# The softplus sum of a hybrid Mamba and RWKV block on TensorE instead of GpSimd and VectorE

## The reference

```
xs, z = split(x @ W_in.T)                         # 512 channels each
xc = silu(conv4(xs) + conv_b)
dt, Bm, Cm = split(xc @ W_x.T, [64, 80])
dt = softplus(dt @ W_dt.T + b_dt)                 # what the change touches
h[t] = exp(dt*A) * h[t-1] + dt * Bm * xc          # 16 states for each of 512 channels
y = (sum_n h*Cm + D*xc) * silu(z);  out = y @ W_out.T
ffn: (silu(x @ Wg.T) * (x @ Wu.T)) @ Wd.T         # 768 hidden
rwkv: e = exp(clip(W + K)); A/B by cumulative sums of e*V and e; (sigmoid(R) * A/B) @ Wo.T
```

## Time and profile before

| | us |
|---|---|
| timed runs (3) | median 1663.07, from 1662.47 to 1665.38 |
| profiled execution, its own time | 1667.68 |
| its span, first to last instruction | 1665.9 |
| TensorE busy in the span | 1518.8 (91%) |
| VectorE | 1467.1 (88%) |
| GpSimd | 1313.8 (79%) |
| ScalarE | 1211.1 (73%) |
| weight loads of TensorE | 748.9 (45%) |

### The profile page before, as it was taken

How to read it: one execution, slowest core, us unless ns; L and a number is a source line. 1 busy time by engine, 2 the same in 40 slices (tenths; PEclk the granted TensorE clock), 3 DMA queues, 4 the chain that set the end, 5 groups by cost and what they waited for, 6 DMA issues and landing times. The chain is left out here.

```text
span 1665.9 us, 19103 instructions
## 1 busy us (share of the span) xinstructions
PE 1518.8 (91%) x5026; PEld 748.9 (45%) x5026; DVE 1467.1 (88%) x1997; ACT 1211.1 (73%) x1993; POOL 1313.8 (79%) x693
## 2 busy tenths in 40 slices
...
GB/s 228 186 202 124 158 150 134 129 151 102 137 153 230 41 128 160 129 207 120 126 159 213 121 119 158 152 183 114 106 155 170 178 88 126 100 57 62 74 45 32
DMA packets 163519, 225.22 MB, mean 135 GB/s; under 512 B 13458, under 2 KB 104083, under 8 KB 163411
## 3 DMA queue, kind: packets, MB, share of 16 engines
...
...
## 5 line engine op out<-in xcount | busy, mean ns | idle before, releaser
L921 POOL TENSOR_TENSOR bu<-rep,bc 128x1024 f32<-128x1024 f32 x256 | 600.4, 2363 | 140.2 <-PE ps_y L1449 65.9
L1085 ACT ACTIVATE ps_d<-rep,scale_a 128x512 f32<-128x512 f32 x512 | 338.4, 684 | 155.1 <-DVE bu L1262 101.1
L1385 PE MATMUL ps_r<-xT,wgu 128*128 128x512 f32 x768 | 351.3, 603 | 7.8 <-ACT xT L1093 2.2
L1255 DVE TENSOR_TENSOR_SCAN ps_d<-ps_d,bu 128x512 f32<-128x512 f32 x272 | 322.6, 1214 | 11.9 <-ACT ps_d L1085 8.3
L927 POOL TENSOR_TENSOR bu<-bu,bc 128x1024 f32<-128x1024 f32 x120 | 282.9, 2363 | 20.1 <-DVE bu L1255 18.9
L1255 DVE TENSOR_TENSOR_SCAN bu<-ps_d,bu 128x512 f32<-128x512 f32 x240 | 285.3, 1209 | 15.0 <-POOL bu L921 10.3
L1385 PE MATMUL ps_r<-mix,wkv 128*128 128x512 f32 x512 | 247.9, 616 | 26.9 <-ACT kv L1122 12.6
L962 ACT ACT_TABLE_LOAD x191 | 245.1, 1283 | 3.4
L1385 PEld LDWEIGHTS ps_r<-xT,wgu 128*128 128x128 f32 x768 | 141.5, 191 | 210.2 <-issue 197.8
L940 POOL TENSOR_TENSOR kv<-sums,kv 128x1024 f32<-128x1024 f32 x64 | 150.7, 2354 | 46.3 <-DVE sums L1352 45.7
L1262 DVE TENSOR_TENSOR bu<-ps_d,bc 128x512 f32<-128x512 f32 x272 | 178.2, 678 | 1.0
...
## 6 DMA issues: line engine op xcount, KB each, us to landing
rep<-dd_scratch SPq DMA_DIRECT2D x128, 512.0 KB, 5.1
...
```

The lines of the kernel that those rows point to most:

```text
L921: pool.tensor_tensor(bu[:, i % BU:i % BU + 2, :], rep[:, g % REP:g % REP + 2, 1, :], bc[:, 0, q, :].unsqueeze(1).to_broadcast([P, 2, T]), ...
L1085: act.activation(ps_d[D_BANK[i]][:, :], rep[:, g % REP, 0, :], ACT.Exp, scale=scale_a[:, a, NQ * j + q:NQ * j + q + 1]).then_inc(decay_rea ...
L1255: dve.tensor_tensor_scan(states, d[:, :], bu[:, i % BU, :], 0.0, ALU.mult, ALU.add)\
L1385: last = pe.matmul(dst, lhs, rhs, start=n == 0, stop=n == len(pairs) - 1)
```

## The change

The three additions leave GpSimd and VectorE. A new unit `p_sum` on TensorE multiplies the four tensors relu(a), e, 1 - u and ln(u) by the identity and accumulates them in the bank that held the `p_dt` of the tile; a new unit `a_sp` on ScalarE copies the bank into the dd slot. GpSimd keeps the product with xc, now for sequence 0 too, and VectorE has no part in dt any more. `a_ln` of the next tile waits for p_sum instead of dt. The bank is released by dt_ready, raised by the copy, instead of sp_relu.

```diff
@@ released
-                "p_xproj": (xdbl_ready, 1), "p_dt": (sp_relu, i + 1),
+                "p_xproj": (xdbl_ready, 1), "p_dt": (dt_ready, i + 1),
@@ GpSimd, g_dt
-                        pool.wait_ge(sp_neg.sem, at(sp_neg, m, i + 1))
-                        pool.tensor_tensor(rest_u, dtx, rest_u, ALU.add).then_inc(sp_rest.sem, 1)
-                        pool.wait_ge(sp_rest.sem, at(sp_rest, m, i + 1))
-                        pool.tensor_tensor(lnu, lnu, rest_u, ALU.add).then_inc(sp_sum.sem, 1)
-                        pool.wait_ge(sp_sum.sem, at(sp_sum, m, i + 1))
-                        pool.tensor_tensor(dt, dt, lnu, ALU.add).then_inc(dt_ready.sem, 1)
                         pool.wait_ge(dt_ready.sem, at(dt_ready, m, i + 1))
                         pool.tensor_tensor(dtx, dt, xc[:, i, :], ALU.mult).then_inc(dtx_ready.sem, 1)
@@ ScalarE, a_ln
-                            act.wait_ge(dt_ready.sem, at(dt_ready, m, i))
+                            act.wait_ge(sp_sum.sem, at(sp_sum, m, i))
@@ ScalarE
+                    elif unit == "a_sp":
+                        act.wait_ge(sp_sum.sem, at(sp_sum, m, i + 1))
+                        act.copy(dd_slot(i)[:, 0, :], ps_r[BANK[m, "p_dt", i]][:, :]).then_inc(dt_ready.sem, 1)
@@ VectorE: the whole of v_dt (three additions and the product) is gone
@@ TensorE
+                    elif unit == "p_sum":
+                        bank = ps_r[BANK[m, "p_dt", i]]
+                        pe.wait_ge(sp_relu.sem, at(sp_relu, m, i + 1))
+                        pe.wait_ge(sp_neg.sem, at(sp_neg, m, i + 1))
+                        for n, part in enumerate((dd_slot(i)[:, 0, :], dd_slot(i)[:, 1, :], rest_u, lnu)):
+                            last = pe.matmul(bank[:, :], ident[:, :], part, start=n == 0, stop=n == 3)
+                        last.then_inc(sp_sum.sem, 1)
@@ ORDER and BANKS: written anew for all five lists; the first words of "p"
-        "hp_turn*2 p_in*7 p_xproj p_dt p_in p_dt*2 p_warm*4 p_dt p_warm*25 hp_turn p_y hp_turn p_in p_y p_in*3 "
+        "hp_turn*2 p_in*7 p_xproj p_dt p_in p_dt*2 p_sum p_dt p_warm*4 p_sum p_warm*6 p_sum p_warm*3 p_y p_sum "
```

More of the change, by code:

```diff
@@ L65 @@
 COUNTS = {
-    "a_dt": JD, "a_in": JD, "a_ln": JD, "a_xc": JD, "a_xproj": 1,  "ha_std": 2, "ha_norm": 2,
+    "a_dt": JD, "g_dt": JD, "p_sum": JD, "a_sp": JD, "a_in": JD, "a_ln": JD, "a_xc": JD, "a_xproj": 1,  "ha_std": 2, "ha_norm": 2,
     "ha_turn": KC, "hp_turn": KC, "hv_stats": 2, "hv_aggr": 2, "p_dt": JD, "p_in": 2 * JD, "p_xproj": 1, "s_dt": JD,
@@ new lines @@
+        "p_warm p_y p_in*3 p_y fp_turn p_warm*4 p_y fp_turn2 fp_turn fp_turn2 p_in*2 p_xproj p_in p_dt p_y p_k "
+        "p_v p_sum p_y p_recept*5 p_k p_dt p_recept p_k p_v p_y p_dt p_sum p_y p_v p_recept*2 p_k p_v p_dt "
+        "p_warm*3 p_k p_y p_sum p_v p_k p_y p_sum p_post p_k p_v p_y p_post p_wo p_wo2 p_wo p_wo2 fp_turn p_v p_y "
+        "fp_turn2 fp_turn fp_turn2 p_k fp_gate fp_up fp_gate fp_up p_y fp_gate p_y fp_up hp_turn fp_gate fp_up "
+        "fp_gate fp_up fp_gate fp_up hp_turn p_v p_in*2 p_y*2 fp_down fp_down2 fp_down fp_down2 p_in*2 p_y p_wo "
@@ new lines @@
+        "fp_gate fp_up p_k fp_gate p_y p_dt fp_up p_v fp_gate fp_up p_sum hp_turn*2 p_y fp_down fp_down2 fp_down "
+        "fp_down2 p_wo p_wo2 p_wo fp_turn fp_turn2 fp_turn fp_turn2 p_wo2 p_y p_in*2 p_y p_k p_in rp_turn "
+        "rp_turn2 p_in rp_turn rp_turn2 p_v p_in p_y p_in*2 p_xproj p_in p_k p_v p_dt p_y p_recept*2 p_sum p_y "
+        "p_recept p_k p_v p_y p_dt p_recept rp_gate p_sum rp_up rp_gate rp_up p_y p_k p_v p_recept rp_gate rp_up "
+        "p_recept rp_gate rp_up p_y rp_gate*2 rp_up p_k rp_up p_y p_v p_recept rp_down rp_down2 p_recept p_y "
```

501 lines of the change are left out of this document (246 added, 255 removed), and 118 rows, old and new, of tables (BANKS, ORDER).

## The result

| | before | after |
|---|---|---|
| median, us (9 runs each) | 1662.47 | 1670.26 |
| lowest to highest | 1658.86 to 1665.38 | 1667.00 to 1676.92 |
| ratio, 95% interval | | 1.0044 [1.0029, 1.0059] |
| profiled execution, its span | 1667.68, 1665.9 | 1671.08, 1669.3 |

The change costs 7.8 us, 0.44%: slower, as forecast, but by a quarter of the 29 us.

What follows compares the result with a forecast made beforehand. TensorE and VectorE were near-bounds in the middle, TensorE alone in the tail. The middle gave +29 us, other terms 0: 1697 on the profiled 1667.7, less 4.6 to the median, 1692 us; range 1660 to 1722.

Steps and rivals of the forecast that it cites:

- The full share: Between the first scans of sequences 1 and 7, TensorE can be busy at most 96.6% of the time.
- The cost of a p_sum instruction: Each p_sum on TensorE is 8 instructions of 512 columns at 0.457 us, 3.66 us.
- its relief worth under 15 us: Taking additions off GpSimd gains below 15 us, as VectorE waits for it 14.1 us in 346 to 1291 us.
- section 8 and tail: From the last first scan to the end: one p_sum meets two fillers and one p_wo2 less, 0, near 374 us.
- TensorE's need in sections 2 to 7: Between first scans of sequences 1 and 7: 1026.8 + 87.8 - 21.6 + 1.8 = 1094.8 us of TensorE work.
- 5 for clock: Taken from TensorE's work in the middle: granted clock was 0.98, a fuller TensorE should lose less; 5 us.
- my own rule: Length of the middle is TensorE's work divided by its reachable busy share: (1094.8 - 5) / 0.966 = 1128 us.
- The start-up, put at 0: Before the first scan: tile 0's chain 2.7 us later, against 3.2 us given back at that scan; 0.
- Sections 0 and 1, put at 0 together: Up to the first scan of sequence 1: removed fillers lay in idle time; 0, between -5 and +5, near 192 us.
- B (banks): Rival: longer-held PSUM banks and p_sum waits keep TensorE at 93.4% or less; +50 to +75, about 1725 us; chance 0.22.
- C (faster): Rival: pipelined TensorE packs closer, is no bound, and GpSimd's relief removes VectorE's waits; -14 us, 1649; chance 0.13.
- the likeliest case: TensorE's added work lengthens the middle: +9 to +49 us, 1672 to 1712; chance 0.58.

## Why the prediction was wrong in size and right in sign

**What was right.** The full share: I took 96.6% of the best section of before, it is 96.4%, and it was not given before: a load of the same size in the old order stayed at 94.7%. That dividing by it gives nearly the measured length is no proof that TensorE sets that length, since with 39 us of products less the length stayed (1105.9 and 1105.7). The cost of a p_sum instruction, the copy (582 ns, forecast 585), GpSimd's 1215 us, its relief worth under 15 us (7.8 when made alone), section 8 and tail (375.1 for 374). VectorE stays at 94.7% of the middle.

**The step that failed: TensorE's need in sections 2 to 7.** I took 1026.8 us as what its existing work needs and added to it: 1094.8 us, less 5 for clock in the length. It is 1067.85, 27 less. By terms, each moment counted once:

| us | forecast | measured |
|---|---|---|
| existing work (995.7 before, 1.8 for p_wo2) | 997.5 | 975.4 |
| p_sum | 24 x 3.66 = 87.8 | 23 x 3.55 = 81.6 |
| fillers (31.2 before, 21.6 removed) | 9.6 | 10.9 |

One more p_sum fell into section 8 than I had counted, and the step from one of its instructions to the next was 0.443 us, not 0.457: 6 us. The existing work is 22. It is elastic. The trace of before has seven stretches at half clock in the middle, 34.1 us in all, with TensorE busy for 29.0 of them; half of that, 14.5, is loss. In them stand 37 instructions with records of over 0.8 us, where 0.59 is usual. After, there is one such stretch, 3.4 us, and no such record. Two rows of TensorE's timeline before, the same four instructions each, and the busy times of the second one's stretch, show it; the first stands behind other work, the second behind 2.00 us of idle time:

```profile
243.83 1.99 PE L1385 MATMUL ps_r<-xnT,win 128*128 128x512 f32 x4
...
266.91 3.37 PE L1385 MATMUL ps_r<-xnT,win 128*128 128x512 f32 x4 [2.00 <-DVE xc L1247]
...
266.91:270.28 3.37, 3.37 (x5) 1.37 (x6) 3.37 (x4) 3.34 (x5) 2.30 (x1) 0.56 0.01 2
```

The granted clock of the second is 0.56: all but its first instruction ran at 1.2 GHz, the lower of the clock's two levels. I had allowed 5 us for clock from the granted 0.98; the rows give 14.5. The remaining 5 to 7 us are, by an estimate, mostly ends of instructions that overlap with nothing when the stream breaks (94 breaks before, 63 after, and a record of 0.59 us against a step of 0.44). The experiments give a series in which the same work costs less the fuller TensorE is:

| kernel | TensorE's share | rest of its work, us | records over 0.8 us |
|---|---|---|---|
| sum for sequences 0, 1 alone | 86.9% | 1018.4 | 120 |
| GpSimd's product four times | 92.2% | 996.9 | 57 |
| before | 93.4% | 995.7 | 37 |
| before, GpSimd lighter | 93.7% | 988.2 | 11 |
| half of the products, conversion ahead | 94.1% | 987.6 | 23 |
| before, TensorE loaded | 94.7% | 985.9 | 16 |
| the change | 96.4% | 975.4 | 0 |
| products twice | 97.1% | 974.1 | 7 |

A part of it was chance: 23 executions of the kernel before had mean granted clocks from 0.971 to 0.981 and took 1657.4 to 1666.4 us; the profiled one had 0.973 and 1667.68. Their median clock is 0.978, and 0.977 on the other two chips; 0.004 to 0.005 of 1666 us is some 7 us of TensorE's time. The nine executions of the change had 0.983 to 0.989, median 0.985, all above the highest of before, and 0.008 more than 0.977 is 13 us. So, as an estimate, some 7 of the 22 us belong to the execution that I read, and most of the rest is what filling TensorE gave back. The same order with TensorE loaded points that way too, with 9.8 us less for its other work. With the measured need, my own rule gives 1067.85 / 0.966 = 1105 us, where 1107.6 was measured; and that need above the present one would have cost time is shown by the doubled sum, 74.0 us for 79.8.

**The start-up, put at 0.** The two terms were about right: tile 0's product ends 3.3 us later (forecast 2.7), the first scan no longer waits for v_dt. The order of VectorE also moved the next sequence's statistics ahead of the first scan and the conversion behind them, and that I didn't price: +7.1 us, 8.6 back when the conversion alone is moved back. It is 2.8 us in the profile of before; I had not asked what would run beside it at its new place.

**Sections 0 and 1, put at 0 together,** are 192.3 before, 186.6 after: in section 1 VectorE has 6.1 us less to do (it has 6.0 more in the middle) and 7.7 us of idle time instead of 14.4. It is no by-product of the late start: with the conversion moved back the section still takes 121.6 us. Why the idle time fell wasn't tested. That two moves which I hadn't priced, +7.1 and -12.8, nearly cancel is luck.

**Rivals.** B (banks) is refuted by the trace of the change: its share is 96.4%, and the waits for the copy of a_sp come to 1.9 us in all. Holding the bank in the old order was not tried. C (faster) would have needed VectorE as the only bound; the need did fall, by 27 of the 55 us that it assumed, but mostly by clock and breaks, not pitch. The chance on the slower side was right; the likeliest case's own range (1672 to 1712) just misses 1670.26, the wide one holds it.

**Where the 29 us went.** The middle grew by 8.3: the existing work gave 22 us, of which I had allowed 5, and the p_sum 6, against 1 for fillers and 2 for a share of 96.4% in place of 96.6%. The same 8.3 can be read from VectorE, which kept its share and has 6.0 us more to do there: 6.0 / 0.947 = 6.3. Half of VectorE's products with C took 46 us from it and gave only 7.7, so neither engine alone explains the length. Outside it, the start-up gave +7.1, section 1 -12.8, the end +0.8: together +3.4 between the profiled executions. The medians differ by 7.8 because the profiled one of before was 5.2 above its median and that of after 0.8. What makes the change affordable seems to be the order written anew: TensorE loaded with 84 us in the order of before costs 65, and 62 with GpSimd relieved; the change, with p_sum less fillers (117 - 55 = 62 us by the forecast's sizes) and GpSimd relieved, costs 7.8. Scaled by 62 / 84, the old order would have asked some 46. That difference is worked out, not measured by itself: the new order with the old sum wasn't run, and the load of that test stands ahead of p_dt, not where p_sum stands.

No version here that computes the full sum is measurably faster than the kernel before. The best is the change with the conversion ahead, 0.9994. Leaving e and 1 - u out with it gives 0.997, and that is another result.
